# Experts' stage of a two-layer transformer kernel: gather by columns in two passes, tokens as f32r high and low parts

## What is computed

```python
grouped = x.reshape(b, s // g, g, d)                       # g = 32 tokens, d = 512
logits = einsum('bntd,des->bntes', grouped, Wc) + bc + tie
perm = (logits == max(logits, axis=-3)).astype(x.dtype)    # the token each (expert, set) takes
permuted = einsum('bntd,bntes->bnesd', grouped, perm)      # gather
inner = relu(einsum('bnesd,esdf->bnesf', permuted, W1) + b1)        # f = 32
result_permuted = einsum('bnesf,esdf->bnesd', inner, W2) + b2
result = einsum('bnesd,bntes->bntd', result_permuted, perm)         # scatter
```

## Time and profile before

| | |
|---|---|
| runs, median of 3 | 2287.25 us (2282.11 to 2287.96) |
| profiled execution | 2278.25 us, its span 2276.5 us |
| TensorE matmul / weight load | 1933.3 us (85%) / 1218.1 us (54%) |
| VectorE / ScalarE / GpSimd | 1358.2 (60%) / 1223.8 (54%) / 666.9 us (29%) |
| DMA | 312.43 MB, mean 137 GB/s |

### The profile page before, as it was taken

One profiled execution on the slowest core, in us unless ns is written; L12 is line 12 of the kernel. 1 busy time (PEld: TensorE's weight loads), 2 busy tenths in 40 slices (PEclk: granted clock), 3 DMA queues, 4 the chain that ended last, 5 costly groups with the idle time before them and its releaser, 6 DMA issues. The chain is left out here.

```text
span 2276.5 us, 41219 instructions
## 1 busy us (share of the span) xinstructions
PE 1933.3 (85%) x14429; PEld 1218.1 (54%) x14467; DVE 1358.2 (60%) x2542; ACT 1223.8 (54%) x2239; POOL 666.9 (29%) x1205
## 2 busy tenths in 40 slices
PE   6999999999999999998496596336699899889875
PEld 3666666666666666665294294114355455446432
DVE  2757666675767667566233333314687786776763
ACT  2666556565665666555022222244776776676853
POOL 1423321322422231240030130003455345345530
PEclk9999999999999999999697697567898998988988
DMA  6424534243443533341547857686536336324200
GB/s 200 137 81 116 149 98 142 73 130 109 134 129 93 154 80 111 82 114 66 135 142 224 254 151 220 249 335 227 167 102 195 113 102 199 114 96 158 66 19 19
DMA packets 201110, 312.43 MB, mean 137 GB/s; under 512 B 30784, under 2 KB 99488, under 8 KB 193632
## 3 DMA queue, kind: packets, MB, share of 16 engines
q1 hardware_dynamic: 141936, 223.49, 31.2%
q10 hardware_dynamic: 42608, 52.97, 7.4%
q0 software_dynamic: 16384, 33.59, 5.7%
HBM read 171.30 MB, written 71.53 MB: 107 GB/s over the span
## 5 line engine op out<-in xcount | busy, mean ns | idle before, releaser
L506 DVE TENSOR_REDUCE a_negmax<-a_score 128x1 f32<-128x512 f32 x512 | 346.1, 684 | 117.2 <-PE a_score L621 109.0
L441 ACT ACTIVATE a_prob<-a_score,a_negmax 128x512 f32<-128x512 f32 x512 | 353.8, 693 | 94.9 <-DVE a_negmax L506 94.0
L317 POOL DMA_DIRECT2D a_q_stack<-a_q_parts x512 | 250.7, 498 | 520.1 <-DVE a_q_parts L500 254.1
L621 PE MATMUL a_score<-a_k_stack,a_q_stack 128*128 128x512 f32 x512 | 354.3, 692 | 9.6 <-ACT a_prob L441 7.8
L629 PEld LDWEIGHTS a_turn<-a_ident,a_prob 128*128 128x128 f32 x2048 | 254.0, 141 | 134.4 <-issue 93.2
L629 PE MATMUL a_turn<-a_ident,a_prob 128*128 128x128 f32 x2048 | 309.1, 274 | 3.4 <-ACT a_perm L417 2.0
L325 ACT COPY a_probT<-a_turn 128x512 f32<-128x512 f32 x256 | 150.0, 586 | 285.7 <-PE a_turn L629 284.0
L325 DVE COPY a_probT<-a_turn 128x512 f32<-128x512 f32 x256 | 176.3, 689 | 212.9 <-PE a_turn L629 212.6
L1943 PE MATMUL c_ff<-c_w2T,c_hqT 128*128 128x512 bf16 x482 | 140.8, 451 | 40.1 <-ACT c_hqT L1479 34.2
L621 PEld LDWEIGHTS a_score<-a_k_stack,a_q_stack 128*128 128x128 f32 x512 | 97.3, 190 | 112.4 <-issue 75.0
L890 PE MATMUL b_work<-b_blocks,b_xn 128*128 128x256 f32 x512 | 128.5, 417 | 24.7 <-POOL b_blocks L862 24.1
(11 more groups left out here) (206 smaller groups left out, 3326.0 us busy)
## 6 DMA issues: line engine op xcount, KB each, us to landing
a_k_stack<-a_k_parts SPq DMA_DIRECT2D x512, 64.0 KB, 2.6
a_q_stack<-a_q_parts POOLq DMA_DIRECT2D x512, 64.0 KB, 2.3
scratch_res<-b_res SPq DMA_DIRECT2D x32, 1024.0 KB, 5.0
c_res<-scratch_res SPq DMA_DIRECT2D x32, 1024.0 KB, 7.6
b_xn<-scratch_xn SPq DMA_DIRECT2D x68, 256.0 KB, 2.7
c_hid<-in_L_ffn_W ACTq DMA_DIRECT2D x16, 1024.0 KB, 8.4
c_negm<-scratch_m SPq DMA_DIRECT2D x64, 256.0 KB, 4.4
a_xs<-in_x ACTq DMA_DIRECT2D x8, 1024.0 KB, 5.2
```

The costliest lines, as they stand in the source:

```text
L317: eng.dma_start(stack[kind][i * DH0:(i + 1) * DH0, M % 2, g, :].bitcast(F32), parts[kind][g * DH0:(g + 1) * DH0, part, :].bitcast(F32)).th ...
L441: nc.scalar.activation(prob[:, U % 4, :], score.bank(U)[:, :], ACT.Exp, bias=negmax[:, u:u + 1], accum_out=sums[:, head_of(U), tile_of(U): ...
L506: nc.vector.tensor_reduce(negmax[:, U % UNITS:U % UNITS + 1], score.bank(U)[:, :], AX.X, ALU.max, negate=True).then_inc(max_ready, 1)
L621: nc.tensor.matmul(score.bank(U)[:, :], stack["Q"][:, M % 2, g, t * P:(t + 1) * P], stack["K"][:, M % 2, g, :], start=True, stop=True).the ...
```

## The change

The two halves of experts become two passes over columns: each pass gathers 256 of the 512 features for all 128 pairs. The first pass's first layer is kept in `part`; the second pass's is added to it, and the second layer then runs once over 32 experts. The tokens' features are stored by the attention phase in the order in which the passes take them. Each tile is split into `high` (its f32r rounding, ScalarE) and `low` (the rest, VectorE), and two f32r matmuls of 512 columns add up in one bank. `blocks` is laid out by DMA: two buffers are zeroed once by VectorE, and four DMAs of 32 partitions put `perm`'s rows into their places. W1 comes in 512 KB a group and pass, in pieces of 256 bytes, with four buffers. Results are evicted into four places of `chosen` which are no longer needed. The core of the diff:

```diff
+                              last = norm1.tile_result(x1.rearrange("p t (q c) -> p t c q", c=C),
+                                                       xn1.rearrange("p t (c q) -> p t c q", c=C), t)
...
+                def load_tokens(h, b):
+                    m = h * B + b
+                    if m >= 2:
+                        work.wait_full(sp, 0, gather_job((m - 1) * T - 1, CH - 1))
+                        sp.wait_ge(low_ready, (m - 1) * T)
                         sp.sem_inc(sp_parted, 1)
+                    sp.dma_start(xn[:, m % 2], tiled(scratch["xn1"])[b, :, :, h * CW:(h + 1) * CW]).then_inc(xn_in[m % 2], 16)
+                    for g in range(GT):
+                        r = slice(g * TG, (g + 1) * TG)
+                        sp.dma_start(blocks[r, m % 2, :, g, :].bitcast(F32), perm_d[b, r]).then_inc(blocks_in[m % 2], 16)
+                def load_w1(h, j):
+                    q = group_job(h, j)
+                    if q >= NW:
+                        aux.wait_full(sp, 0, q - NW)
...
+                for b in range(2, B):
+                    if b - 2 < NW:
+                        load_w1(0, b - 2)
+                    load_tokens(0, b)
+                load_tokens(1, 0)
+                load_tokens(1, 1)
+                for j in range(NW, GROUPS):
+                    load_w1(0, j)
+                for j in range(NW):
+                    load_w1(1, j)
+                for b in range(2, B):
+                    load_tokens(1, b)
...
+                    for c in range(CH):
+                        j = gather_job(n, c)
+                        work.wait_free(pe, 0, j)
+                        for tile in (high, low):
+                            last = nc.tensor.matmul(work.bank(j)[:, :], tile[:, n % 2, c * P:(c + 1) * P],
+                                                    blocks[:, m % 2, t].rearrange("p g e -> p (g e)"), start=tile is high, stop=tile is low)
...
+            def out_of_gather(eng, copy, n, c):
+                j = gather_job(n, c)
+                work.wait_full(eng, 0, j)
+                g = n % TILES * GT
+                copy(chosen[:, c, :, g:g + GT], work.bank(j)[:, :].rearrange("p (g e) -> p e g", g=GT)).then_inc(work.free[j % 4], 1)
...
+                def split_high(n):
+                    m, t = n // T, n % T
+                    if t == 0:
+                        act.wait_ge(xn_in[m % 2], (m // 2 + 1) * 16)
+                    if n >= 2:
+                        work.wait_full(act, 0, gather_job(n - 2, CH - 1))
+                    nc.scalar.copy(high[:, n % 2, :], xn[:, m % 2, t, :]).then_inc(high_ready, 1)
+                def inner_values(j):
+                    q = group_job(1, j)
+                    aux.wait_read(act, 0, q)
+                    for e in range(NE):
+                        nc.scalar.activation(inner[:, q % 2, e, :], part[:, j * NE + e, :], ACT.Relu,
+                                             bias=b1c[:, j * NE + e:j * NE + e + 1]).then_inc(relu_done, 1)
...
+                for h in range(PASSES):
+                    for n in range(h * TILES, (h + 1) * TILES):
+                        split_high(n)
+                        if n > h * TILES:
+                            out_of_gather(act, nc.scalar.copy, n - 1, 1)
...
+                for j in range(GROUPS + 1):
+                    if j < GROUPS:
+                        inner_values(j)
+                    if j >= 1:
+                        for e in range((j - 1) * NE, j * NE):
+                            if e + 2 < EXP:
+                                load_w2(e + 2)
+                            for s in (0, 2):
+                                out_of_second(act, nc.scalar.copy, e, s)
...
+                for k in range(2):
+                    nc.vector.tensor_copy(blocks[:, k].rearrange("p t g e -> p (t g e)"), zero[:, :].to_broadcast([P, T * GT * ES])).then_inc(zeroed, 1)
+                def split_low(n):
+                    m, t = n // T, n % T
+                    dve.wait_ge(high_ready, n + 1)
+                    nc.vector.tensor_tensor(low[:, n % 2, :], xn[:, m % 2, t, :], high[:, n % 2, :].bitcast(F32), ALU.subtract
+                                            ).then_inc(low_ready, 1)
+                def add_group(j):
+                    q = group_job(1, j)
+                    aux.wait_full(dve, 0, q)
```

More of the change, by code:

```diff
@@ L812, in _ @@
-                load_tokens(0, 0)
[L813 to L826, removed]
-                        if e % NE == 0 and e // NE + 2 < GROUPS:
-                            load_w1(e // NE + 2)
-                        for s in range(SETS):
-                            work.wait_read(sp, h * WORK + GATHERED, 4 * e + s)
-                        sp.dma_start(res_d[h, e], res[:, e % 2]).then_inc(res_stored[e % 2], 16)
@@ new lines, in _ @@
+                load_tokens(1, 0)
[6 more added lines that the diff above has]
+                    load_tokens(1, b)
+                for e in range(EXP):
+                    if e % NE == 0 and e // NE + NW < GROUPS:
+                        load_w1(1, e // NE + NW)
+                    for s in range(SETS):
+                        work.wait_read(sp, 0, second_job(e, s))
+                        if s % 2 == 1:
+                            sp.sem_inc(sp_parted, 1)
+                    sp.dma_start(res_d[e], results(e)).then_inc(res_stored[e % NR], 16)
@@ L838, in _ @@
+                for k in range(NR):
+                    sp.wait_ge(res_stored[k], 16 * EXP // NR)
             @block.gpsimd
@@ new lines, in turn_w2, with second_layer @@
+                def turn_w2(e):
+                    pe.wait_ge(w2_sorted, e + 1)
+                    wt.wait_free(pe, 0, e)
+                    for c in range(C):
+                        last = nc.tensor.transpose(wt.bank(e)[:, c * P:(c + 1) * P], w2s[:, e % 2, c, :], ident[:, :])
+                    last.then_inc(wt.full[e % 2], 1)
+                def second_layer(e):
+                    q = group_job(1, e // NE)
+                    if e % NE == 0:
+                        pe.wait_ge(inner_ready, e // NE + 1)
+                    wt.wait_read(pe, 0, e)
+                    pe.sem_inc(pe_parted, 1)
+                    for s in range(SETS):
+                        work.wait_free(pe, 0, second_job(e, s))
+                        if s % 2 == 1:
+                            pe.sem_inc(pe_parted, 1)
+                    for s in range(SETS):
+                        j = second_job(e, s)
+                        r = slice(s * F, (s + 1) * F)
+                        nc.tensor.matmul(work.bank(j)[:, :], inner[r, q % 2, e % NE, :], w2T[r, e % 2, :],
+                                         start=True, stop=True).then_inc(work.full[j % 4], 1)
```

303 lines of the change are left out of this document (135 added, 168 removed).

## The result

The changed kernel takes 2250.04 us, median of four runs (2246.42 to 2255.49), against 2287.61 us for the kernel before (2282.11 to 2290.71): a ratio of 0.985, 95% interval 0.982 to 0.988. The change saves 37.6 us, where 10.5 were forecast. The profiled execution took 2248.99 us with a span of 2247.2.

A forecast was written before the change was run, and what follows sets the result against it. Bounds: TensorE and a 16 us stall in each gather, W2's load round trip in the layers. Stage 9.5+55.1+21+54.6+7.5+186 = 333.7 against 345.7, +1.5 ahead: -10.5, so 2267.7 profiled, 2277 us median; range 2248 to 2312.

The forecast's parts named there:

- rival A: Whole kernel faster: inner values cost nothing, intervals stay at 5.62 us, tiles run at 1.44: 2249 us; chance 0.22.
- three signs of being wrong: Gather's period off 1.69 us by more than 0.3; W1 holds tokens back; result evictions keep the old pace.
- the tile's pace: Both gathers: split, matmul and eviction through two buffers take 1.69 us a tile instead of 1.87.
- the stage between the passes: First layer of pass 0, nearly all DMA for W1 groups 4 to 7: about 21 us (16 to 31).
- halfway price for reads 128 elements apart: Gather evictions from PSUM: middle between no cost (1.57 us a tile) and 1.57 times slower reads (1.82).
- half clock for 30% of the time: Gather matmuls: full clock 70% of the time, between 1.44 and 1.87 us a tile, giving 1.57.
- Rival C: Gathers slower: strided PSUM reads at 1.57 times, TensorE at its lower clock throughout, tile 2.03: 2299 us; chance 0.18.
- The stall of 16 us a half: Each gather before: token loads stand behind W1 on SP's queue; the change removes these 16 us.
- W1 at 3.2 us a group: W1 loads in 256-byte pieces: 3.2 us a group, between 2.8 by bytes and 5.4 unchanged.
- Rival B: W1 loads slower: 256-byte packets cost what 512-byte ones do, +30 us, 2307 us; chance 0.18.
- Zeroing: Start of the stage: two VectorE copies of 2048 columns, 2.0 to 2.4 us each, hold back SP's token loads.
- Second layer, 186 forecast: Last part, 31 intervals: inner values delay the W2 load, +3.7 us a group, 24.0 per four experts; 186 us (170 to 200).

The follow-up runs named there:

- Experiment 2: Kernel before, with the four W1 loads of each half put one by one between token batches 1 to 4: 2268.59 us, ratio 0.9929.
- Experiment 8: Changed kernel with the first two W2 loads issued behind the second pass's fifth and sixth tile, or twenty-first and twenty-second: 2254.22 and 2251.85 us.
- experiment 5: Changed kernel with ScalarE's inner values (ReLU) of the next group moved behind the evictions of the present one: 2243.19 us, ratio 0.9816.
- experiment 4: Changed kernel with each W1 group loaded by one DMA of 128 partitions instead of two of 64, same 256-byte pieces: 2247.12 us, ratio 0.9828.

## Why the prediction was right in its sign and short in size

The forecast said 2277 us, the time is 2250. The sign was right; the gain is 37.6 us where 10.5 were forecast. That 2250.04 lies within the range of 2248 to 2312 is luck by 2 us: the range reaches that low only for rival A, and the forecast's own, 2262 to 2292, is missed by 12. Of the three signs of being wrong that the prediction names, the first has come: the tile's pace differs from 1.69 us by 0.35, more than 0.3. The second came in part, since W1 held the blocks of three batches back by 1.1 to 1.7 us. The third nearly came: results are evicted every 5.77 us, closer to the 5.62 of the kernel before than to the forecast's 6.0.

In the profile's own terms it missed 18.7 us (2267.7 forecast, 2249.0 measured): gathers 18.0 too long, second layer 7.2, start 1.2; against that 3.6 too little between the passes, 0.4 in the start of the last part, and 3.7 in the untouched tail. The other 8 us are the step from profile to median, 9 us assumed and 1 found.

Some sums of the prediction don't come out of their terms. The start's terms give 9.6 to 10.4 us, not 9.5; the stage between the passes 22.2, not 21; the start of the last part 8.0, not 7.5 (7.9 measured). The tile's upper value of 1.82 is the plain mean of 1.60 and 2.03; with the 70% that the prediction gives the full clock it is 1.73, and the middle 1.65 instead of 1.69, which is 2.6 us less in 64 tiles. Together these slips all but cancel.

- **The tile's pace, 1.69 forecast and 1.34 measured, is the failed step.** Its chain was right (1.44 at full clock, and TensorE waits for `b_low` in the rows). Three additions were not. The halfway price for reads 128 elements apart (0.12 a tile, 0.04 of it the slip above) is nothing: 684 and 587 ns. The half clock for 30% of the time (0.13) came only in the first two or three tiles of each gather; behind them 1.00 is granted. The remaining 0.10 is the matmul chain: 0.23 us a piece as forecast, though that was read behind a matmul of another kind, but the 0.19 of the first weight load is hidden, since it starts just 0.03 us ahead of its matmul (1236.39 and 1236.42). For the first two the forecast's own lower bound was the true value, and it took middles; the row nearest in kind, the same engines copying from the same banks, was the better guide than the copy into `w2T`, whose step lies in SBUF on the writing side.
- **The Trainium skill's rule** (SBUF — State Buffer, section Door 1: The DMA port swizzle) says of PSUM's 8-byte lines that non-contiguous access slows matmuls; the prediction carried it over to copies. In these copies by VectorE and ScalarE it does not show (684 and 587 ns). Rival C rested on it and on the lower clock throughout; neither came.
- **The stall of 16 us a half** was judged rightly: batches no longer wait 4 us. Experiment 2 gives 16 of the 32 us by order alone. The prediction fitted W1 and a batch of tokens into a batch of 6.8 us, but a batch takes 5.4, so 4.1 us of short waits came back.
- **W1 at 3.2 us a group** is 3.05 by three successive first layers (1182.80, 1185.82, 1188.91). 16 x 3.05 / 2048 is 24 ns a packet against 42.3 for twice the bytes. Rival B is refuted. By the rule in the Trainium skill (DMA: Bandwidth & Descriptors, section Specifications) pieces under 512 bytes lose line rate; at this size the trace shows a loss of a tenth, 171 GB/s against the 190 of the 512-byte pieces, both in DMAs of 64 partitions.
- **Zeroing,** forecast 2.0 to 2.4 us a copy, took 1.27 with 2048 columns. The scaling from 512 columns at 599 ns was wrong. With 0.7 us ahead of the copies the tokens are issued 3.2 us after the start instead of 4.0 to 4.8, and the first matmul follows 5.05 us later (5.6 by the forecast's terms).
- **Between the passes** the forecast left out ScalarE's four issues ahead of its first split, 3.06 us; with the slip of 1.2 in its sum that is more than the 3.6 that the part is longer. Experiment 8 adds that moving them gains nothing.
- **Second layer, 186 forecast and 178.8 measured.** That a delay recurs in every group was right; its size was not. The 5.4 us are the way from an eviction to the issue in a group at the lower clock (5.43); 0.7 to 0.8 of it is there in the kernel before, and other groups are shorter, so the load is delayed by 3.2 to 4.7 us. It costs 2.0 to 2.3 a group instead of 3.7: 22.6 for four experts without a W1 load, against 20.6 in experiment 5 and the forecast's 20.3 (4 x 5.07). A W1 load costs 3.0 where 1 was assumed. These errors nearly cancel: the first 24 experts took 144.75 us (1247.51 to 1392.26), 24.1 for four, where the forecast has 24.0 and four W1 loads of 1. About half of the 7.2 us that are missing is a count: seven delays for six, since the ReLU of the first two groups precedes every result, 3.7 us.
- **Rival A** gave 2249, one microsecond off, and that is luck: in the profile's terms it is 9 us too low (2239.7 against 2249.0), which the step from profile to median, 8 us less than assumed, makes up for. It has half the reason: its tile of 1.44 without the two middles is nearer the 1.34, while the inner values do cost something, though only where no W1 load covers them. Its 5.62 us an interval, against 178.8 / 31 = 5.77 measured, is near because the kernel before paid for W1 loads in its intervals too.

Open is what gives the higher rate of experiment 4. That W1 covers the ReLU's wait rests on the intervals of three kernels; no kernel without both was run, and the groups that have neither are the late ones of experiment 5.

## What to carry to other kernels

When a load's buffer comes free only when its consumer is done, count the round trip first. Here two more buffers gave 52 us, more than the change itself, and the traffic limit became visible only after that. Two delays that fall on the same load are not a sum; take away each alone before pricing them. And a pause on the compute engines may be what gives a saturated DMA queue its time, so look at the DMA share inside the pause before closing it.

## What the runs showed of the hardware

- VectorE and ScalarE read PSUM 128 elements apart at the speed of plain reads (684 and 587 ns for 128x512), while the copy that writes SBUF with a step of four still takes 1.07 us (1068 ns mean of 30).
- f32r matmuls of 128x128 by 512 columns start 0.23 us apart at granted clock 1.00 (1236.73, 1236.96, 1237.19) and 0.43 apart just behind the pause between the passes (1196.43, 1196.85, 1197.28), in a window (1189 to 1199) with 0.83 granted, a mix of both levels.
- TensorE kept granted clock 1.00 through 40 us of a gather in which it worked 30 of them, and had 0.71 in the last part at 51 of 100.
- A VectorE conversion of a broadcast column to 2048 f32r columns takes 1.27 us, not four times a 512-column copy of 599 ns.
- Pieces of 256 bytes in DMAs of 64 partitions moved at 166 GB/s, of 128 partitions (and half as many DMAs) at 208, in the same 10 us of two kernels.
